# A two-layer recommendation tower on one core: scratch clears between the gathers of the second half, other waits before gathers, W1's gathers moved

## The chip, the core and the metric

The kernel runs on one core of one Trainium2 chip. A core has a matrix engine (TensorE, PE in the profile), a vector engine (DVE), a scalar engine (ACT), GpSimd (POOL) and a queue for plain transfers (SP). Each engine works through its own instructions in order and meets the others through semaphores: an instruction raises one when it is done, and a wait on another engine holds that engine until the count is there. Gathers (indirect DMAs) are issued by POOL and carried out by DMA engines. The metric is the time of one execution in microseconds, as the median of several.

## What is computed

```
e = stack([tbl_f[ids[:, f]] for f in 0..31], axis=1)        # (1024, 32, 64)
xi, xj = e[:, idx_i, :], e[:, idx_j, :]                      # the 496 pairs i < j
left = einsum('bpd,pde->bpe', xi, W)                         # W: (496, 64, 64)
z = sum(left * xj, axis=-1)                                  # (1024, 496)
h = concatenate([z, dense_ctx], axis=1)                      # (1024, 512)
h = maximum(h @ W_top1 + b_top1, 0)                          # 512 -> 512
h = maximum(h @ W_top2 + b_top2, 0)                          # 512 -> 256
y = h @ W_top3                                               # (1024, 1)
```

All values are fp32. Each of the 1024 samples looks up one row of 64 values in each of 32 tables; every pair of fields is combined through its own 64 by 64 matrix; three dense layers follow.

## The kernel before

**Tiling.** The batch is cut into four quarters of 256 samples, two tiles of 128 samples each. The 32 fields are taken as 16 field pairs m = 15 down to 0. A field pair of a quarter needs four gathers (two fields, two tiles; line 625), each of 128 rows of 256 bytes, one row to a partition. So there are 64 gathers to a quarter and 256 in all, counted 0 to 255 here. PE turns the gathered rows over (line 805, four matmuls for a field pair in the profile: every fp32 matmul stands there as two), and ACT copies the result from PSUM to `X` (line 720), two field pairs at a time over most of the program.

**Pieces.** The pair products are made in 248 pieces, 62 to a quarter. A column piece is 8 matmuls of PE at line 840 and one multiply of DVE (line 684 or 680); a row piece is 4 matmuls at line 845 and one multiply at line 692; an "own" piece (2 to a quarter) is 16 matmuls at line 853 and two multiplies at line 672. PE writes a piece to one of three double banks of `left`; DVE reads it, and each multiply raises `multiplied`. PE can be at most three pieces ahead of DVE. Column products are summed by PE (line 866, in turns of eight), row products by ACT (line 737, 16 activations with their reads of the accumulator), by DVE (line 701) or, after the last gather, by POOL (line 642, six steps).

**Dense layers.** Once a quarter's sums are there, its transposes (line 823), four steps of layer 1 (line 884), layer 2 (906) and layer 3 (915) are put in between the pieces of the next quarter; those of the last quarter close the program. Layer 1 needs `W1`, whose rows are also gathered, by four indirect DMAs (line 614) that stand before gather 64.

**What sets the order.** A planner (`Order`) walks through a model of the engines with the constants at the top of the file and writes down one list of steps; every engine issues its part of that list in order. The planner's model of the gathers (`landed`) decides when it takes a field pair.

**What holds the gathers.** Before gather g, POOL waits until `pieces_before(g)` pieces are multiplied: `int((g - 32) * 0.95)` from gather 64 on (in the first quarter also another line, half a piece per gather from gather 16 on, and a limit through the field pairs). So gather 122 waits for 85 pieces, gather 128 for 91, gather 255 for 211. At the start of the third and the fourth quarter POOL also waits for all products two quarters back, since the buffer `rows` holds two quarters.

```
for q in range(QUARTERS):
    if q >= 2:
        pool.wait_ge(multiplied, work_of_quarter[q - 2])
    if q == 1:
        pool.wait_ge(index_loaded, 16)
        for c in range(CHUNKS):
            pool.indirect_dma_start(out=w1_sb[:, c, :], ...)
```

## Time and profile before

| what | value |
|---|---|
| median of 3 runs | 525.97 us (525.26 to 527.53) |
| the profiled execution, its own time | 524.06 us |
| its span (first to last instruction) | 521.9 us |
| PE busy / DVE busy / ACT busy / POOL busy | 423.1 / 336.6 / 337.3 / 279.0 us |
| PE's mean granted clock | 0.935 of full speed |
| gathers | 256, first at 3.4 us, last at 452.1 us |

The profile is one execution. "Busy" is the time in which an engine had an instruction running; for PE the ends are modelled. A wait is put down to the instruction whose semaphore ended it; "issue" stands for a wait that nothing in the profile explains, and "remote" or "another core or an unknown queue" for one whose releaser the profile could not name (there is only one core here). The 2.2 us between span and time lie before the first instruction and after the last.

### The profile page before, as it was taken

The page shows a single profiled execution, that of the slowest core. Times are in us where ns is not written, and L with a number is a line of the kernel's source. Part 1 is how long each engine was busy: PE and PEld are TensorE (multiplying, and loading weights), DVE is VectorE, ACT ScalarE, POOL GpSimd, SP SyncE. Part 2 cuts the span into 40 slices and gives each one's busy share as a digit, 9 for nine tenths or more (in the row PEclk, how much of TensorE's full clock was granted, in tenths as well). Part 3 has the DMA queues.
Part 4 walks back from the last instruction along what each step waited for, and adds up shares of the span by engine and source line. Part 5 has one row for each costly group of instructions (what it writes and reads, how often), then busy time and mean ns, then how long its engine had stood idle before and what let it go on. Part 6 is the DMA issues. An engine that isn't in the chain of part 4 may idle for free.

```text
span 521.9 us, 8845 instructions
## 1 busy us (share of the span) xinstructions
PE 423.1 (81%) x2440; PEld 217.9 (42%) x2440; DVE 336.6 (64%) x293; ACT 337.3 (65%) x2511; POOL 279.0 (53%) x326
## 2 busy tenths in 40 slices
PE   0056697977987879799898897999969788899998
PEld 0033243433534425354444443554424334445546
DVE  0014484666767869376858776787866688698870
ACT  0003584767777867666695786668573897599472
POOL 6747365655646455255455555554455555686510
PEclk9996697979888999799898999999889999999999
DMA  7999900120100010000000000010001000000000
GB/s 136 170 167 166 141 21 20 37 76 22 24 16 21 16 25 15 12 19 23 16 21 20 21 21 22 18 21 21 16 18 23 19 18 18 19 2 1 1 1 1
DMA packets 44680, 18.87 MB, mean 36 GB/s; under 512 B 39764, under 2 KB 40280, under 8 KB 44632
## 3 DMA queue, kind: packets, MB, share of 16 engines
q1 hardware_dynamic: 36120, 8.86, 13.2%
q0 software_dynamic: 8512, 9.45, 8.3%
q8 instruction: 20, 0.33, 0.3%
q14 instruction: 28, 0.23, 0.2%
HBM read 18.29 MB, written 0.00 MB: 35 GB/s over the span
## 4 chain that ended last, share of the span: by engine, by line
PE 50%; ACT 15%; issue 11%; another core or an unknown queue 10%; DVE 9%; POOL 3%; DMA 2%; DVEq 0%; ACTq 0%
PE left L840 15%; PE left L845 15%; ACT row_products L737 14%; PE z_sum L866 9%; PE turned L884 4%; DVE row_products L692 4%; DVE column_products L684 3%; POOL rows L625 3%; PE turned L805 2%; PE turned L906 2%; DVE column_products L672 1%; PE left L884 1%; DMA rows<-in_tbl_dram,ids_sb 1%; ACT X L720 1%
## 5 line engine op out<-in xcount | busy, mean ns | idle before, releaser
L625 POOL DMA_INDIRECT rows<-in_tbl_dram,ids_sb x256 | 242.2, 946 | 204.4 <-issue 64.2
L737 ACT ACTIVATE row_products<-row_products 128x64 f32<-128x64 f32 x1216 | 291.4, 244 | 27.7 <-issue 16.1
L737 ACT ACTIVATION_READ_ACCUMULATOR row_products<-row_products 128x1 f32 x1216 | 231.5, 190 | 20.8 <-issue 19.8
L684 DVE TENSOR_TENSOR column_products<-left,X 128x1024 f32<-128x1024 f32 x104 | 125.1, 1218 | 95.5 <-PE left L840 54.3
L692 DVE TENSOR_TENSOR row_products<-left,rows 128x1024 f32<-128x1024 f32 x120 | 143.1, 1217 | 52.9 <-PE left L845 32.0
L840 PE MATMUL left<-X,w_sb 64*128 64x256 f32 x960 | 138.5, 416 | 26.4 <-DVE row_products L692 8.6
L845 PE MATMUL left<-w_sb,X 64*128 64x512 f32 x480 | 134.9, 658 | 25.1 <-DVE column_products L672 7.9
L840 PEld LDWEIGHTS left<-X,w_sb 64*128 64x128 f32 x960 | 96.3, 201 | 82.9 <-issue 33.3
L866 PE MATMUL z_sum<-column_products,ones_window 128*32 128x512 f32 x512 | 78.7, 661 | 8.3 <-issue 3.9
L845 PEld LDWEIGHTS left<-w_sb,X 64*128 64x128 f32 x480 | 43.3, 197 | 71.7 <-issue 39.4
L720 ACT ACTIVATE X<-turned 128x512 f32<-128x512 f32 (+1 forms) x34 | 19.2, 565 | 77.1 <-issue 27.3
L805 PE MATMUL turned<-ident,rows 128*128 128x128 f32 x128 | 23.4, 307 | 33.9 <-DMA rows<-in_tbl_dram,ids_sb 30.7
L866 PEld LDWEIGHTS z_sum<-column_products,ones_window 128*32 128x32 f32 x512 | 16.5, 118 | 57.6 <-issue 38.0
L701 DVE TENSOR_REDUCE z_nat<-row_products 128x16 f32<-128x1024 f32 x34 | 40.2, 1209 | 0.1
L642 POOL TENSOR_TENSOR row_products<-row_products 128x512 f32<-128x512 f32 (+4 forms) x50 | 30.4, 607 | 12.0 <-DVE row_products L692 8.9
L805 PEld LDWEIGHTS turned<-ident,rows 128*128 128x128 f32 x128 | 14.6, 151 | 52.4 <-issue 49.0
L770 ACT ACTIVATE h<-turned,b_sb 128x256 f32<-128x256 f32 x18 | 7.5, 470 | 30.9 <-PE turned L906 16.0
L672 DVE TENSOR_TENSOR column_products<-left,X 64x1024 f32<-64x1024 f32 x16 | 19.5, 1220 | 12.2 <-remote 9.0
L680 DVE TENSOR_TENSOR column_products<-left,X 128x1024 f32<-128x1024 f32 x16 | 19.5, 1218 | 8.2 <-remote 5.5
L884 PE MATMUL turned<-z,w_sb 128*128 128x256 f32 x96 | 24.0, 393 | 0.0
L884 PEld LDWEIGHTS turned<-z,w_sb 128*128 128x128 f32 x96 | 17.3, 191 | 10.4 <-issue 8.5
L853 PE MATMUL left<-X,w_sb 64*64 64x256 f32 x128 | 17.1, 383 | 1.2 <-issue 1.2
(30 smaller groups left out, 79.5 us busy)
## 6 DMA issues: line engine op xcount, KB each, us to landing
rows<-in_tbl_dram,ids_sb POOLq DMA_INDIRECT x256
w_sb<-in_W_top_dram SPq DMA_DIRECT2D x1, 512.0 KB, 5.6
w_sb<-in_L_rec_W_dram SPq DMA_DIRECT2D x1, 496.0 KB
w_sb<-in_L_rec_W_dram SPq DMA_DIRECT2D x1, 480.0 KB
w_sb<-in_L_rec_W_dram SPq DMA_DIRECT2D x1, 464.0 KB
w_sb<-in_L_rec_W_dram SPq DMA_DIRECT2D x1, 448.0 KB
w_sb<-in_L_rec_W_dram SPq DMA_DIRECT2D x1, 432.0 KB
w_sb<-in_L_rec_W_dram SPq DMA_DIRECT2D x1, 416.0 KB
```

The source lines that it names most:

```text
L625: pool.indirect_dma_start(out=rows[:, q % 2 * QT + t, f * D:(f + 1) * D], out_offset=None, in_=tables[f], in_offset=bass.IndirectOffsetOnA ...
L642: ins = nc.gpsimd.tensor_tensor(to, of[:, :, 0:d], of[:, :, d:2 * d], ALU.add)
L672: ins = nc.vector.tensor_tensor(to[part].rearrange("p o (g b) -> p (o g) b", b=QB), of[part].rearrange("p o (g b) -> p (o g) b", b=QB), X[ ...
L684: nc.vector.tensor_tensor(to, of, X[:, n:n + 2, :].rearrange("p g b -> p (g b)").unsqueeze(1).to_broadcast([P, 2, BANK]), ALU.mult).then_i ...
L692: nc.vector.tensor_tensor(row_products[:, n % ROW_PRODS, :, :], left[:, s, :, :], rows[:, t:t + 1, 2 * D * c:2 * D * (c + 4)].to_broadcast ...
L701: nc.vector.tensor_reduce(z_nat[:, x[2] % (2 * QT), column:column + 16], row_products[:, n % ROW_PRODS, :, :].rearrange("p o (j d) -> p (o ...
L737: ins = nc.scalar.activation(product, product, ACT.Copy, accum_out=z_nat[:, tile, column:column + 1])
L805: ins = nc.tensor.transpose(turned[:, column:column + P], rows[:, q % 2 * QT + t, 2 * D * m:2 * D * (m + 1)], ident[:, :])
L840: ins = nc.tensor.matmul(left[:, s, odd, QB * g:QB * (g + 1)], weights(odd, m, k, 2), X[D * odd:D * odd + D, q % 2 * FP + m, :], start=Tru ...
L845: ins = nc.tensor.matmul(left[:, s, odd, :], X[D * odd:D * odd + D, q % 2 * FP + m, P * t:P * (t + 1)], weights(odd, m, c, 8), start=True, ...
L866: nc.tensor.matmul(z_sum[32 * r:32 * r + 32, :], ones_window[:, 30 - 2 * t:62 - 2 * t], column_products[:, v // 2 % COLUMN_PRODS, v % 2, : ...
L884: ins = nc.tensor.matmul(bank, w1_sb[:, c, n * P:(n + 1) * P], z[:, c, :], start=(begins and c == chunks[0]), stop=(ends and c == chunks[-1]))
```

## The change

**Clears between gathers.** From gather 128 on, POOL clears a scratch tile `pause` of 128 partitions by 320 fp32 columns before every gather, and waits for its own clear to be done (`paused`) before it goes on. The tile is read by nobody. There are 128 such clears.

**Waits before gathers.** `pieces_before` now follows `int((g - 44) * 1.02)`. Gather 64 waits for 20 pieces (30 before), gather 96 for 53 (60), gather 128 for 85 (91), gather 192 for 150 (152), gather 224 for 183 (182), gather 255 for 215 (211).

**W1.** Its four gathers stand one by one before gathers 96, 100, 104 and 108.

**The planner's constants.** A work step costs it 0.83 (0.85), a row sum on DVE 1.3 (1.23) and on ACT 4.0 (3.9), a gather 1.6 from gather 128 on; slack, margin and the spacing of dense layers change. With that the order of the steps on all engines changes; the arithmetic and the number of matmuls and products do not.

```diff
-MLP_APART = 4
-X_WAIT, MLP_WAIT = 10, 16
+MLP_APART = 8
+X_WAIT, MLP_WAIT = 10, 12
-WORK, ... = 0.85, ...
-MULTIPLY, ROWSUM_DVE, ROWSUM_ACT, ... = 1.23, 1.23, 3.9, ...
+WORK, ... = 0.83, ...
+MULTIPLY, ROWSUM_DVE, ROWSUM_ACT, ... = 1.23, 1.3, 4.0, ...
-ACT_SLACK, DVE_SLACK, MARGIN, ... = 0.5, 0.6, 1.0, ...
+ACT_SLACK, DVE_SLACK, MARGIN, ... = 0.5, 1.0, 0.1, ...
-GROUP, AHEAD, APART, LAG = 1, 32, 0.95, 3
+GROUP, AHEAD, APART, LAG = 1, 44, 1.02, 3
+W1_BEFORE = [96, 100, 104, 108]
+PAUSED, PAUSE, PITCH = 128, 320, 1.6
...
-            self.gathered.append(begin + GATHER)
+            self.gathered.append(begin + (GATHER if g < PAUSED else PITCH))
...
-                if q == 1:
-                    pool.wait_ge(index_loaded, 16)
-                    for c in range(CHUNKS):
-                        pool.indirect_dma_start(out=w1_sb[:, c, :], ...).then_inc(w1_loaded, 16)
                 for m in range(FP - 1, -1, -1):
                     for n in range(4):
-                        before = pieces_before(first_gather(q, m) + n)
+                        t, f, g = n // 2, 2 * m + n % 2, first_gather(q, m) + n
+                        if g in W1_BEFORE:
+                            c = W1_BEFORE.index(g)
+                            if c == 0:
+                                pool.wait_ge(index_loaded, 16)
+                            pool.indirect_dma_start(out=w1_sb[:, c, :], ...).then_inc(w1_loaded, 16)
+                        if g >= PAUSED:
+                            nc.gpsimd.memset(pause[:, :], 0.0).then_inc(paused, 1)
+                            pool.wait_ge(paused, g - PAUSED + 1)
+                        before = pieces_before(g)
                         if before:
                             pool.wait_ge(multiplied, before)
```

In the changed file lines 614, 625 and 642 are 627, 638 and 655, and lines 805, 840, 845, 853, 866, 884, 906 and 915 are 818, 853, 858, 866, 879, 897, 919 and 928.

On POOL, from the start of the gathers to the end of the program, this stood before (the last six rows are one row sum, of which there are ten):

```order
L625 DMA rows<-in_tbl_dram,ids_sb 128x64 x64
L614 DMA w_sb<-in_W_top_dram,w_index_sb 128x512 x4
L625 DMA rows<-in_tbl_dram,ids_sb 128x64 x192
L642 TENSOR_TENSOR row_products<-row_products 128x16x32
L642 TENSOR_TENSOR row_products<-row_products 128x16x16
L642 TENSOR_TENSOR row_products<-row_products 128x16x8
L642 TENSOR_TENSOR row_products<-row_products 128x16x4
L642 TENSOR_TENSOR row_products<-row_products 128x16x2
L642 TENSOR_TENSOR z_nat<-row_products 128x16
```

and this stands there now, up to the second gather that has a clear before it:

```order
L638 DMA rows<-in_tbl_dram,ids_sb 128x64 x96
L627 DMA w_sb<-in_W_top_dram,w_index_sb 128x512
L638 DMA rows<-in_tbl_dram,ids_sb 128x64 x4
L627 DMA w_sb<-in_W_top_dram,w_index_sb 128x512
L638 DMA rows<-in_tbl_dram,ids_sb 128x64 x4
L627 DMA w_sb<-in_W_top_dram,w_index_sb 128x512
L638 DMA rows<-in_tbl_dram,ids_sb 128x64 x4
L627 DMA w_sb<-in_W_top_dram,w_index_sb 128x512
L638 DMA rows<-in_tbl_dram,ids_sb 128x64 x20
L632 MEMSET pause 128x320
L638 DMA rows<-in_tbl_dram,ids_sb 128x64
L632 MEMSET pause 128x320
```

The W1 gathers are spread, each gather from 128 on has its clear, and at the end POOL keeps six row sums of ten.

On PE, around the last turning of gathered rows in the program, the order was:

```order
L866 MATMUL z_sum<-column_products,ones_window 32x512 x8
L884 MATMUL turned<-z,w_sb 128x256 x4
L840 MATMUL left<-X,w_sb 128x256 x4
L845 MATMUL left<-w_sb,X 128x512 x4
L805 MATMUL turned<-ident,rows 128x128 x4
L840 MATMUL left<-X,w_sb 128x256 x4
L845 MATMUL left<-w_sb,X 128x512 x6
L805 MATMUL turned<-ident,rows 128x128 x4
L840 MATMUL left<-X,w_sb 128x256 x4
L845 MATMUL left<-w_sb,X 128x512 x4
L866 MATMUL z_sum<-column_products,ones_window 32x512 x8
```

and is now:

```order
L919 MATMUL turned<-h,w_sb 128x256 x4
L858 MATMUL left<-w_sb,X 128x512 x2
L853 MATMUL left<-X,w_sb 128x256 x4
L858 MATMUL left<-w_sb,X 128x512 x2
L818 MATMUL turned<-ident,rows 128x128 x4
L853 MATMUL left<-X,w_sb 128x256 x4
L879 MATMUL z_sum<-column_products,ones_window 32x512 x8
L853 MATMUL left<-X,w_sb 128x256 x4
L858 MATMUL left<-w_sb,X 128x512 x4
L853 MATMUL left<-X,w_sb 128x256 x4
L928 MATMUL turned<-h,w_sb 1x256 x2
```

The last turning, which needs gather 255, stood behind 220 pieces and stands behind 228; the third quarter's layers 1 and 2 (884 and 906, now 897 and 919), of which two steps and all of layer 2 stood behind it, now stand ahead of it.

On ACT, at the end of the program, 16 activations being one row sum, the order was:

```order
L737 ACTIVATE row_products,z_nat<-row_products 128x64 x32
L770 ACTIVATE h<-turned,b_sb 128x256 x2
L737 ACTIVATE row_products,z_nat<-row_products 128x64 x16
L791 ACTIVATE y<-turned 1x256
L737 ACTIVATE row_products,z_nat<-row_products 128x64 x32
L755 ACTIVATE z<-turned 128x512
```

and is now:

```order
L750 ACTIVATE row_products,z_nat<-row_products 128x64 x16
L733 ACTIVATE X<-turned 128x512
L750 ACTIVATE row_products,z_nat<-row_products 128x64 x16
L804 ACTIVATE y<-turned 1x256
L750 ACTIVATE row_products,z_nat<-row_products 128x64 x80
L768 ACTIVATE z<-turned 128x512
```

The last unbroken stretch of row sums on ACT grows from two to five. Over the program ACT has 79 of the 120 row sums (76 before), DVE 35 (34) and POOL 6 (10).

## Rows read from the trace of the kernel before

**Rows 1.** The page: busy times of the engines, and the shares of the chain.

```profile
PE 423.1 (81%) x2440; PEld 217.9 (42%) x2440; DVE 336.6 (64%) x293; ACT 337.3 (65%) x2511; POOL 279.0 (53%) x326
...
PE 50%; ACT 15%; issue 11%; another core or an unknown queue 10%; DVE 9%; POOL 3%; DMA 2%; DVEq 0%; ACTq 0%
```

**Rows 2.** Busy time by stretch; the first line names the columns.

```profile
core 0: us, PE busy (x) PEld busy (x) DVE busy (x) ACT busy (x) POOL busy (x), PEclk, DMA share, GB/s
72.40:117.00 44.60, 36.33 (x176) 16.04 (x172) 27.69 (x25) 29.30 (x216) 27.44 (x29) 0.85 0.16 42
...
210.70:452.10 241.40, 211.34 (x1270) 107.75 (x1272) 171.13 (x149) 171.06 (x1281) 125.77 (x133) 0.96 0.09 19
452.10:506.40 54.30, 53.20 (x324) 28.51 (x322) 49.28 (x43) 42.68 (x330) 33.22 (x61) 1.00 0.01 2
```

**Rows 3.** DVE's waits, 210.7 to 452.1 us: total us, times, longest us.

```profile
DVE column_products L684 <- remote: 10.8, 4, 3.4
DVE column_products L672 <- remote: 9.0, 2, 4.6
DVE row_products L692 <- remote: 8.5, 3, 4.7
```

**Rows 4.** Timeline of POOL from 376 us: start, length, instruction, idle before it.

```profile
376.39 0.95 POOL L625 DMA_INDIRECT rows<-in_tbl_dram,ids_sb  x1 [4.07 <-DVE row_products L692]
...
382.63 0.94 POOL L625 DMA_INDIRECT rows<-in_tbl_dram,ids_sb  x1 [0.30 <-issue]
387.73 0.95 POOL L625 DMA_INDIRECT rows<-in_tbl_dram,ids_sb  x1 [4.15 <-DVE column_products L672]
```

**Rows 5.** Timeline of DVE in the same stretch.

```profile
379.43 1.22 DVE L692 TENSOR_TENSOR row_products<-left,rows 128x1024 f32<-128x1024 f32 x1
385.00 2.46 DVE L672 TENSOR_TENSOR column_products<-left,X 64x1024 f32<-64x1024 f32 x2 [4.36 <-remote]
```

**Rows 6.** Timeline of PE in the same stretch.

```profile
379.00 1.95 PE L853 MATMUL left<-X,w_sb 64*64 64x256 f32 x16
...
387.51 1.71 PE L845 MATMUL left<-w_sb,X 64*128 64x512 f32 x4 [4.05 <-DVE column_products L672]
```

**Rows 7.** Timeline of POOL from 251 us, the first and last of seven gathers.

```profile
251.94 0.94 POOL L625 DMA_INDIRECT rows<-in_tbl_dram,ids_sb  x1 [2.73 <-DVE row_products L692]
...
261.48 0.94 POOL L625 DMA_INDIRECT rows<-in_tbl_dram,ids_sb  x1 [0.30 <-issue]
```

**Rows 8.** Timeline of POOL: gathers 122 and 255, and the first sum.

```profile
210.73 0.95 POOL L625 DMA_INDIRECT rows<-in_tbl_dram,ids_sb  x1 [1.23 <-DVE column_products L684]
...
452.14 0.95 POOL L625 DMA_INDIRECT rows<-in_tbl_dram,ids_sb  x1 [2.82 <-DVE column_products L684]
453.11 3.32 POOL L642 TENSOR_TENSOR row_products<-row_products 128x512 f32<-128x512 f32 x5
```

**Rows 9.** Groups of POOL by shape: count, busy us, mean ns, idle before them.

```profile
L642 POOL TENSOR_TENSOR row_products<-row_products 128x512 f32<-128x512 f32 x10 | 12.7, 1272 | 8.9 <-DVE row_products L692 8.9
...
L604 POOL TENSOR_SCALAR_AFFINE_SELECT ident<-ident 128x128 f32<-128x128 f32 x1 | 0.3, 285 | 0.2 <-POOL ident L602 0.2
L602 POOL MEMSET ident<- 128x128 f32 x1 | 0.2, 205 | 0.3 <-POOLq L947 0.3
```

**Rows 10.** Groups of PE, 210.7 to 452.1 us: count, busy us, mean ns.

```profile
L840 PE MATMUL left<-X,w_sb 64*128 64x256 f32 x512 | 71.0, 401 | 15.9 <-DVE column_products L684 4.7 <-ACT X L720 4.3 <-DVE column_products L680 3.1
L845 PE MATMUL left<-w_sb,X 64*128 64x512 f32 x240 | 66.0, 640 | 11.3 <-DVE column_products L672 4.7 <-ACT X L720 4.5 <-DVE column_products L684 0.8
L866 PE MATMUL z_sum<-column_products,ones_window 128*32 128x512 f32 x286 | 41.9, 652 | 3.8 <-DVE column_products L672 2.4 <-DVE column_products L684 1.5
```

**Rows 11.** The same groups, 452.1 to 506.4 us.

```profile
L845 PE MATMUL left<-w_sb,X 64*128 64x512 f32 x80 | 20.0, 608 | 0.0
L840 PE MATMUL left<-X,w_sb 64*128 64x256 f32 x112 | 15.0, 389 | 0.6 <-DVE column_products L672 0.6
L866 PE MATMUL z_sum<-column_products,ones_window 128*32 128x512 f32 x60 | 7.9, 600 | 1.5 <-DVE column_products L684 1.5
```

## What I expect of the change, before it was run

> **What bounds the kernel now.** I read the page first [rows 1]: PE is busy for 423 of 521.9 us and leads the chain with 50%, but 10% of the chain are waits whose releaser has no name, on a program that has one core. So PE is the bound in part, and something that is not work takes the rest. The table by stretch [rows 2] says where. From gather 122 to gather 255 (210.7 to 452.1 us) PE stands idle for 241.4 - 211.3 = 30.1 us and DVE is busy for 71% of the time. After the last gather (452.1 to 506.4 us), with the same kinds of pieces, PE is idle for 1.1 of 54.3 us and DVE is 91% busy. What differs is that no gathers are issued.
>
> The waits of DVE in the stretch [rows 3] hold 28.3 us in nine waits without a named releaser, of up to 4.7 us. One of them, close up: POOL issues six gathers with only 0.30 us between them, from 376.39 to 382.63 us [rows 4]. PE has finished an own piece at 380.95 us [rows 6], DVE has been free since 380.65, and yet DVE begins that piece at 385.00 [rows 5], 2.4 us after the last gather of the run began. PE, its banks full, starts again at 387.51 and has lost 4 us. PE's signal was there late, not its work. Seven gathers that come as four and three, with a gap between, bring no wait of this kind [rows 7]: they take 9.5 us from first to last start, where seven at the run's pitch of 1.25 us take 7.5. My reading: a long unbroken run of gathers holds back the signals of the other engines until the run has landed, and a gap within it prevents that.
>
> **The clears: what they cost POOL.** The trace has no clear of 320 columns. The one of 128 columns took 0.205 us [rows 9]; if all of that grows with the columns, 320 take 0.51 us, and if most of it is fixed, little over 0.2. A two-input sum of 512 columns took 1.272 us, so at its rate 320 would take 0.80: an upper bound from a dearer kind. I take 0.37. A POOL instruction follows a gather 0.02 us later (452.14 + 0.95 to 453.11) [rows 8]; one that waits for a POOL instruction's signal starts 0.2 us after it [rows 9], and a gather 0.30 us after another [rows 4]: I take 0.28 from a clear to its gather. A gather takes 0.95. The pitch is then 0.95 + 0.02 + 0.37 + 0.28 = 1.62 us, with ends of 1.43 and 2.05. Queued behind each clear is only the next gather, and later POOL's row sums; PE waits for gathers at its turnings. 127 pitches of 1.62 are 206 us, and the stretch now takes 241, so the pace has room.
>
> **What the clears give back.** They turn every run into single gathers with 0.67 us between them. If that ends the held signals, the stretch falls to what PE needs. From above: its busy time as it stands, at the tail's share of 98%, 211.3/0.98 = 215.7 us. From below: the matmuls of the stretch are dearer than those of the tail [rows 10, 11], because PE's issue was slowed and its granted clock was 0.96 rather than 1.00 [rows 2]. At the tail's price lines 840, 845 and 866 would save 71.0 - 512 x 15.0/112 = 2.4, 66.0 - 240 x 20.0/80 = 6.0 and 41.9 - 286 x 7.9/60 = 4.2 us: 198.7/0.98 = 202.8 us. The middle is 209, POOL's own pace is 206, and I add 2 for signals that are still held: 211, a saving of **30.4 us** (25.7 to 38.6). DVE alone, at the 91% of its tail, would need 171.1/0.908 = 188.6; it isn't next. ACT isn't either, with 171.1 busy of 241.4.
>
> **The waits before gathers.** The threshold falls by 6 to 10 pieces between gathers 64 and 128, which no work needs: PE waited for a gather's landing only near the start. In the first half nothing is put between gathers, so earlier release means longer runs. From 72.4 to 117 us POOL has 29 instructions, busy for 27.4 of 44.6 us, and PE is idle for 8.3 us [rows 2]. With the new thresholds POOL finds nearly every wait fulfilled there and about 36 gathers follow on each other. W1's four, a pitch of 1.25 us each, leave this stretch, which gives 5 us of it back; they move to places where POOL waits for pieces anyway, and layer 1 comes 20 pieces after the fourth. Bounds: nothing, or 12 us if PE's idle share there more than doubles. I take **+3 us**. From gather 192 on the thresholds are within four pieces of the old ones. The last gather waits for 215 pieces rather than 211, but the turning that needs it moved from piece 220 to 228, so the lead is 13 pieces, about 19 us, against a landing of 2.4.
>
> **The order.** PE has the same matmuls. Four row sums leave POOL: ACT gets three, of about 3.8 us each, DVE one. Before gather 255 both have time. At the end ACT has five row sums in a row, 19 us, beside 20 pieces at 54.3/37 = 1.47 us, 29 us; that hides, and costs 12 us at most if ACT is late with all. I take **+1 us**, for the last of them before the quarter's transposes. Dense layers in other places cost what they cost before.
>
> **The sum**, against the profiled execution: 521.9 - 30.4 + 3 + 1 = 495.5 us of span; 2.2 us around it make 497.7. The median lies 1.9 us above the profiled execution, so **499.5 us**.
>
> **A rule against this.** DVE's wait of 4.36 us ends with the gathers' landing, not with any work of PE [rows 4 to 6]. The Trainium skill (SBUF — State Buffer, section "SBUF: two separate sides") says that engine ports and DMA ports are disjoint and that a compute operation and a DMA cannot slow each other. By that rule the clears would give nothing and the time would be that of the first rival. The trace disagrees with it at least as far as signals go: 4.36 us without a named releaser in a run of gathers, and none after 452 us. The rival stays for the chance that the common cause is another.
>
> **Rivals.**
> 1. *The number of gathers counts, not the gap.* In a stretch of 241.4 us there are 133 of POOL's gathers, one in 1.8 us; afterwards they come at 1.62 when PE is fast, so the signals would be held as often, only at other places. Against it: the four and three gathers above. Then only the costs stay, 525.97 + 4 = 530 us, or 527 if one or two of the holds go.
> 2. *The clear's own signal is held.* POOL now waits for a signal 128 times. If a hold catches it, the next gather begins only when the last has landed: 2.4 + 0.3 = 2.7 us instead of 1.62. Gathers then bound the end: gather 128 at 210.7 + 3, 127 pitches, 2.4 for landing, 20 pieces of 1.47 with 1 for the turning, 15.5 from the last product to the end: 262 + 127p, and with the 4.1 us above 266.1 + 127p. It decides from p = 1.84 on, and equals the old time at p = 2.05, when 39% of the clears are held. With every second one held, p = 2.16 and the time is 540 us: slower. A clear at the two-input rate (p = 2.05) alone gives the old time. For it: all engines' signals seem to be held, POOL's wait of 4.15 us included [rows 4]. Against: single gathers hold nothing in the trace.
> 3. *The first half's runs cost 12 us, not 3.* 508.5 us, still faster.
> 4. *The clear hides in the gap.* The 0.30 us between gathers may be the sequencer's, beside which a clear costs little; the pitch is then 1.43 and the change does half of what it says: 499.5 + 15 = 514.5 us.
>
> **Chances.** My forecast 0.69, with a range of its own of 488 (38.6 saved, the first half at nothing) to 510 (25.7 saved, ACT's sums at 7); rival 1 0.12; rival 2 0.06; rival 3 0.08; rival 4 0.05. A measurement of this kernel can tell 0.5%, 2.6 us, from no change. Forecast, rivals 3 and 4 and a sliver of rival 1 are faster: 0.83. Rival 1 between 523.3 and 528.6 and a mild rival 2 are the same: 0.07. The rest is slower: 0.10. For 8 in 10 the range has to reach into rival 3 and 4 above, and to a stretch of about 200 us below: 485 to 521.
>
> **What would show it.** Right: starts of gathers from 128 on at 1.55 to 1.75 us; DVE's waits without a releaser in the second half under 8 us instead of 28.3; PE idle under 12 us between the gates at 85 and 211 pieces; the granted clock near 1.00. Wrong: the same holds at the new pitch (rival 1), gaps of over 1.5 us between a clear and its gather without a wait for DVE (rival 2), or PE waiting at its turnings for gathers. If the first half's PE idle time grows by over 8 us, rival 3 was in play.

## The result, and the profile after

| | before | after |
|---|---|---|
| median of 4 runs | 525.86 us (525.26 to 527.53) | 491.04 us (490.39 to 491.57) |
| the profiled execution / its span | 524.06 / 521.9 us | 491.57 / 489.8 us |
| after over before | | 0.9333, 95% interval 0.9307 to 0.9358 |

The changed kernel is faster by 6.7%. The forecast was 499.5 us with a range of 485 to 521; the time lies in the range, 8.5 us below the forecast.

The page of after, first the busy times, the clock by slices, the clears and the last line of the chain (busy us, mean ns, idle before them), against [rows 1]:

```profile
PE 400.6 (82%) x2440; PEld 213.8 (44%) x2440; DVE 336.6 (69%) x294; ACT 344.3 (70%) x2607; POOL 314.8 (64%) x430
...
PEclk9995698677999797999999999999999999999999
...
PE 46%; ACT 5%; issue 2%; DVE 2%; DVEq 0%; ACTq 0%
...
L632 POOL MEMSET pause<- 128x320 f32 x128 | 48.4, 378 | 0.1
```

The 10% of the chain without a named releaser are gone, PE is busy for 22.5 us less with the same 2,440 matmuls, and its clock stays up once the clears have begun. Busy time by stretch, for [rows 2] (us of the stretch, then the engines, granted clock, DMA share, GB/s):

```profile
72.40:117.00 44.60, 22.25 (x124) 11.72 (x122) 19.80 (x17) 21.95 (x160) 26.54 (x29) 0.73 0.11 21
...
225.70:438.00 212.30, 207.31 (x1330) 113.80 (x1328) 188.10 (x165) 184.16 (x1427) 168.69 (x255) 1.00 0.11 21
438.00:474.40 36.40, 34.98 (x240) 18.50 (x240) 33.22 (x29) 32.88 (x264) 20.32 (x37) 1.00 0.01 3
```

Between gather 128 (225.76 us) and gather 255 (437.99) PE now idles for 5.0 us, at clock 1.00. The first half went the other way: from 72.4 to 117 us PE idles for 22.4 us, where it was 8.3. DVE's waits between those two gathers, for [rows 3]:

```profile
DVE row_products L705 <- PE left L858: 12.3, 13, 3.3
DVE column_products L697 <- PE left L853: 5.2, 7, 1.2
DVE row_products L705 <- issue: 4.3, 3, 3.8
```

No "remote" is left among them. POOL's timeline there, for [rows 4] (start, length, idle before):

```profile
376.00 0.95 POOL L638 DMA_INDIRECT rows<-in_tbl_dram,ids_sb  x1 [0.27 <-DVE row_products L705]
376.95 0.38 POOL L632 MEMSET pause<- 128x320 f32 x1
377.60 0.95 POOL L638 DMA_INDIRECT rows<-in_tbl_dram,ids_sb  x1 [0.27 <-POOL pause L632]
378.56 0.38 POOL L632 MEMSET pause<- 128x320 f32 x1
379.45 0.95 POOL L638 DMA_INDIRECT rows<-in_tbl_dram,ids_sb  x1 [0.51 <-DVE column_products L697]
```

Three pitches of 1.60 and one of some 1.88 repeat; the mean is 212.23/127 = 1.671 us. PE's groups from 225.7 to 438 us, for [rows 10, 11]:

```profile
L858 PE MATMUL left<-w_sb,X 64*128 64x512 f32 x270 | 68.6, 609 | 3.2 <-ACT X L733 1.6 <-issue 1.5
L853 PE MATMUL left<-X,w_sb 64*128 64x256 f32 x512 | 67.3, 389 | 0.0
L879 PE MATMUL z_sum<-column_products,ones_window 128*32 128x512 f32 x272 | 32.7, 598 | 0.0
```

The means of 609, 389 and 598 ns are those of the old tail (608, 389, 600), where the old stretch had 640, 401 and 652.

By the pieces at which DVE stands, the 32.1 us of span came from these stretches:

| stretch | before | after | difference | forecast |
|---|---|---|---|---|
| start to piece 85 | 210.5 | 225.0 | +14.5 | +3 |
| piece 85 to piece 211 | 241.4 | 197.5 | -43.9 | -30.4 |
| piece 211 to the end | 70.0 | 67.3 | -2.7 | +1 |

What the first half lost can be seen in one place. The old thresholds no longer break the run, and 14 gathers follow on each other. POOL, then DVE:

```profile
90.36 0.94 POOL L638 DMA_INDIRECT rows<-in_tbl_dram,ids_sb  x1 [3.58 <-DVE column_products L697]
...
106.58 0.94 POOL L638 DMA_INDIRECT rows<-in_tbl_dram,ids_sb  x1 [0.30 <-issue]
```

```profile
94.83 1.21 DVE L714 TENSOR_REDUCE z_nat<-row_products 128x16 f32<-128x1024 f32 x1
110.27 3.49 DVE L705 TENSOR_TENSOR row_products<-left,rows 128x1024 f32<-128x1024 f32 x3 [14.23 <-remote]
```

DVE stands for 14.23 us and goes on 2.7 us after the last of the 14 has left POOL: the wait of [rows 5], three times as long. The size of this loss varies. The same steps up to piece 85 took 219.2, 216.3 and 220.6 us in the traces of a1, m1 and e4 below, on chips 7 and 8.

### The profile page after: what moved, and what is told of

Read it like the earlier page. It is cut to its first block, busy times and chain, and to the rows that moved or that the text cites. A ratio compares the mean times of both kernels' runs of the same rounds, so it can differ in the third digit from the quotient of the medians.

```text
span 489.8 us, 9169 instructions
## 1 busy us (share of the span) xinstructions
PE 400.6 (82%) x2440; PEld 213.8 (44%) x2440; DVE 336.6 (69%) x294; ACT 344.3 (70%) x2607; POOL 314.8 (64%) x430
## 4 chain that ended last, share of the span: by engine, by line
PE 46%; ACT 5%; issue 2%; DVE 2%; DVEq 0%; ACTq 0%
PE left L858 13%; PE left L853 13%; PE z_sum L879 7%; PE turned L897 4%; ACT row_products L750 4%; PE turned L919 2%; PE turned L818 2%; PE left L897 1%; PE left L866 1%; PE turned L928 1%; PE left L919 1%; DVE row_products L705 1%; DVE z_nat L714 0%; DVE column_products L685 0%; ACT X L733 0%
## 5 line engine op out<-in xcount | busy, mean ns | idle before, releaser
L750 ACT ACTIVATE row_products<-row_products 128x64 f32<-128x64 f32 x1264 | 302.5, 244 | 24.3 <-issue 13.6
L750 ACT ACTIVATION_READ_ACCUMULATOR row_products<-row_products 128x1 f32 x1264 | 241.0, 191 | 11.8 <-issue 11.8
L705 DVE TENSOR_TENSOR row_products<-left,rows 128x1024 f32<-128x1024 f32 x120 | 143.3, 1218 | 54.6 <-PE left L858 20.2
L697 DVE TENSOR_TENSOR column_products<-left,X 128x1024 f32<-128x1024 f32 x104 | 125.0, 1218 | 74.1 <-PE left L853 46.4
L853 PE MATMUL left<-X,w_sb 64*128 64x256 f32 x960 | 137.0, 415 | 35.8 <-DVE row_products L705 18.9
L858 PE MATMUL left<-w_sb,X 64*128 64x512 f32 x480 | 128.3, 630 | 15.8 <-DVE column_products L697 12.2
L853 PEld LDWEIGHTS left<-X,w_sb 64*128 64x128 f32 x960 | 94.9, 201 | 92.7 <-issue 32.0
L879 PE MATMUL z_sum<-column_products,ones_window 128*32 128x512 f32 x512 | 64.9, 613 | 1.0 <-DVE column_products L697 1.0
L632 POOL MEMSET pause<- 128x320 f32 x128 | 48.4, 378 | 0.1
L714 DVE TENSOR_REDUCE z_nat<-row_products 128x16 f32<-128x1024 f32 x35 | 41.9, 1209 | 0.0
L879 PEld LDWEIGHTS z_sum<-column_products,ones_window 128*32 128x32 f32 x512 | 13.9, 110 | 36.1 <-issue 29.6
L655 POOL TENSOR_TENSOR row_products<-row_products 128x512 f32<-128x512 f32 (+4 forms) x30 | 18.2, 606 | 8.2 <-DVE row_products L705 6.2
```

What stands on the lines that cost most here:

```text
L632: nc.gpsimd.memset(pause[:, :], 0.0).then_inc(paused, 1)
L697: nc.vector.tensor_tensor(to, of, X[:, n:n + 2, :].rearrange("p g b -> p (g b)").unsqueeze(1).to_broadcast([P, 2, BANK]), ALU.mult).then_i ...
L705: nc.vector.tensor_tensor(row_products[:, n % ROW_PRODS, :, :], left[:, s, :, :], rows[:, t:t + 1, 2 * D * c:2 * D * (c + 4)].to_broadcast ...
L714: nc.vector.tensor_reduce(z_nat[:, x[2] % (2 * QT), column:column + 16], row_products[:, n % ROW_PRODS, :, :].rearrange("p o (j d) -> p (o ...
L750: ins = nc.scalar.activation(product, product, ACT.Copy, accum_out=z_nat[:, tile, column:column + 1])
L853: ins = nc.tensor.matmul(left[:, s, odd, QB * g:QB * (g + 1)], weights(odd, m, k, 2), X[D * odd:D * odd + D, q % 2 * FP + m, :], start=Tru ...
```

## Experiments

A measure that I use below is the **late start**: DVE's start of a piece less the later of PE's last matmul of that piece and DVE's own last end, both from the timeline, summed over all pieces where it is above 0.8 us. Behind gather 128 (so behind 227.3 us) it is 47.7 us before and nothing after; ahead of it, from 30 us on, it is 47.2 us before and 60.1 after. It is more than the waits marked "remote", since many of these waits stand in the views under PE's name: they ended with a signal of PE that had been raised, but came late.

That it is the signal that comes late, and not DVE that fails to take it, the semaphore records of the trace show. The piece of [rows 5] ends on PE at 380.94 us, its signal is recorded at 384.98, and DVE starts at 385.00. In all 39 late starts of before, DVE starts 23 to 25 ns behind the record of a signal of PE. Of the recorded piece signals of PE, 80 of 226 come more than 0.15 us behind PE's last matmul in before, 35 of 205 in after, and none of them behind gather 128. ACT's are late too (18 of 65 row sums in before). DVE's never are, in no trace of the first kind below (251 recorded in before), nor are the signals of the 128 clears in after.

One thing has to be known to read the numbers. **The kernel before took 520 to 526 us in three sets of runs and 426 to 427 us in three others.** The second three were on three chips (1, 13 and 14). Of the first three, two were on chips 7 and 8; the chip of the first comparison is not on record and may be one of them or a third. I call them the first and the second kind. Chips 1, 7, 8, 13 and 14 each stand in one such set only, so the kind may belong to the chip or to its state at that time. Each ratio is to runs of before on the same chip.

**No clears.** The changed kernel's whole plan without the clears, first on two chips of the second kind, then on one of the first.

```
-                        if g >= PAUSED:
-                            nc.gpsimd.memset(pause[:, :], 0.0).then_inc(paused, 1)
-                            pool.wait_ge(paused, g - PAUSED + 1)
```

> The changed kernel with its 128 clears taken out and nothing else: its order of steps, its waits before gathers and the places of W1's gathers stay. My theory (unbroken runs of gathers hold back the engines' signals, and the clears break the runs): the gathers from 128 on come at 1.25 us again in runs, DVE's waits without a named releaser return in the second half (none now, 28 us in the kernel before), and the time goes from 491 to 515-535 us. Rival (the gain came from the new order and the new waits, the clears only keep POOL busy): 488-495 us.

> The changed kernel without its clears again, in the hope of a chip that holds signals (the first such run came to a chip where the kernel before took 427 us and says nothing on holds). If the kernel before takes over 500 us here: by my theory the time is 515-535 us, its own loss in the second half 30 us or more of DVE waits without a releaser; if order and waits made the gain, 485-495 us. If the kernel before takes 427 us: 427 again.

> The changed kernel's plan with all 128 clears left out (the pause tile is never written; the computation is the same). The kernel before takes about 521 to 526 us on one kind of chip and about 427 us on another; both cases are stated. Where before takes over 500 us: theory (the clears end the held signals of the second half, so without them the holds come back from the 128th gather on): 515 to 530 us, with sums of late VectorE starts of some 40 us behind the 128th gather. Rival (the order of the work and the steeper waits did it, not the clears): 485 to 495 us, as the changed kernel. Where before takes about 427 us: 427 within 0.5 per cent by both, as measured already on two such chips.

| run | this | before, same chip | ratio (95%) |
|---|---|---|---|
| e1_no_clears (second kind) | 427.08 | 426.72 | 1.0023 (0.9997 to 1.0048) |
| n1_no_clears (second kind) | 427.26 | 426.37 | 1.0023 (0.9998 to 1.0048) |
| m1_no_clears (first kind) | 512.12 | 520.41 | 0.9828 (0.9765 to 0.9892) |

On the second kind no signal is late (in e1 none of 248 piece signals of PE is recorded more than 0.15 us behind its matmul), and both kernels take the same time. POOL in e1, two rows of a run of 23 gathers at 1.25 us:

```profile
180.10 0.94 POOL L635 DMA_INDIRECT rows<-in_tbl_dram,ids_sb  x1 [0.30 <-DVE column_products L694]
...
207.57 0.94 POOL L635 DMA_INDIRECT rows<-in_tbl_dram,ids_sb  x1 [0.30 <-issue]
```

All of DVE's waits of 1 us and more in sum, of that run's whole span:

```profile
DVE column_products L694 <- PE left L850: 43.0, 17, 31.3
DVE row_products L702 <- PE left L855: 27.1, 27, 5.7
DVE column_products L690 <- PE left L850: 1.6, 2, 1.2
DVE column_products L682 <- PE left L863: 1.0, 2, 0.6
```

There is no "remote" anywhere. On the first kind, m1 has the held signals back behind gather 128. Its waits of DVE there (217.1 to 446.6 us), and one place of POOL and of DVE:

```profile
DVE column_products L694 <- remote: 6.5, 3, 2.9
...
DVE column_products L690 <- remote: 4.7, 2, 3.1
DVE row_products L702 <- remote: 3.0, 1, 3.0
```

```profile
429.81 0.95 POOL L635 DMA_INDIRECT rows<-in_tbl_dram,ids_sb  x1 [0.47 <-issue]
...
433.56 0.95 POOL L635 DMA_INDIRECT rows<-in_tbl_dram,ids_sb  x1 [0.31 <-issue]
```

```profile
430.30 2.35 DVE L694 TENSOR_TENSOR column_products<-left,X 128x1024 f32<-128x1024 f32 x2
435.50 1.23 DVE L694 TENSOR_TENSOR column_products<-left,X 128x1024 f32<-128x1024 f32 x1 [2.85 <-remote]
```

This run is of four gathers only. The kernel before has such places too: after two gathers and a gap of 0.69 us come three, and DVE starts 2.44 us late, POOL and then DVE:

```profile
342.09 0.94 POOL L625 DMA_INDIRECT rows<-in_tbl_dram,ids_sb  x1 [0.69 <-issue]
...
344.58 0.95 POOL L625 DMA_INDIRECT rows<-in_tbl_dram,ids_sb  x1 [0.30 <-issue]
```

```profile
346.52 1.22 DVE L684 TENSOR_TENSOR column_products<-left,X 128x1024 f32<-128x1024 f32 x1 [2.44 <-PE left L840]
```

So a run need not be long to hold a signal, and one gap of 0.69 us between short runs does not always prevent it.

The expectation of m1 had 515 to 530 us by my theory and 485 to 495 by the rival, that order and thresholds did it all. 512.1 is just outside mine, and 17 us from the rival's: 17 late starts between gathers 128 and 255 with 33.4 us in sum (I had said some 40). So on the first kind the order, the thresholds and W1's places bring 1.7% by themselves (interval 1.1 to 2.4%), and the clears, by the difference of the ratios to before (0.9828 - 0.9338, the latter from the next run), 4.9% or 25.5 us; the two ratios come from two chips, each good to 0.7%. The mean pitch of m1's gathers behind gather 128 is (446.56 - 217.08)/127 = 1.807 us; with clears it is 1.671. The gathers come more densely with the clears and hold nothing: the mean rate and the number are excluded as the cause. What stays as the cause is the spacing from one gather to the next. Whether it acts as a gap or as the short pitch within a run (1.25 us against 1.60) the runs do not part, since both changed together.

Three kernels have a trace on each kind, and there the late starts (from 30 us on) can be set beside the difference of the spans: m1 and e1, the same program, 89.9 us of late starts for 81.6 us of span; after and a2, 60.1 for 53.8; m3 and e3 (below), 13.1 for 6.7. The held signals are enough for the whole distance between the kinds.

**The changed kernel again,** on a chip of the first kind and on one of the second.

> The changed kernel itself, run beside the kernel before on the chip of this batch. In the first comparison the kernel before took 526 us and its signals were held in runs of gathers; on the chip of the four runs above it took 427 us and none was held. If this chip is like the first: 491 us against 526. If it is like the second: POOL's pace alone sets the second half. Gather 128 is issued at about 171 us (as in the kernel without clears), 127 pitches of 1.67 us end at 383, and 2.4 + 20 x 1.47 + 16.5 us behind them give a span of 431 us: 431-436 us against 427, a change that is slower by 1-2%. Rival (the clears also free PE there): 425 us or less.

> The changed kernel itself beside the run before it. Where before takes over 500 us: 484 to 492 us again, which makes it the third chip of that kind. Where before takes about 427 us: no hold there to be ended, so only the price of the clears is left: the 128th gather near 172 us, 127 x 1.67 us behind it the last at 384 to 386 us, 436 to 440 us, slower than before by 2 to 3 per cent. The other view (the steeper waits and the order are worth their 8 us there too) has 426 to 431 us.

a1: 486.07 us against 521.28, ratio 0.9338 (0.927 to 0.9406), with the same picture: no late start behind gather 128, 56.0 us ahead of it. a2: 437.89 against 425.94, ratio 1.0284 (1.0262 to 1.0305), as expected (436 to 440). The row of the stretch from gather 128 to 255, of a2 and below it of e1 (no clears):

```profile
171.60:384.00 212.40, 198.43 (x1258) 108.09 (x1256) 177.41 (x155) 174.97 (x1355) 168.84 (x255) 0.98 0.11 21
```

```profile
171.40:364.60 193.20, 189.09 (x1223) 103.69 (x1216) 171.18 (x150) 167.97 (x1303) 119.76 (x128) 1.00 0.12 23
```

Where no signal is held the clears can give nothing; the gathers' pace of 1.67 us takes 212.4 us instead of 193.2, and PE is left with 14 us of idle time instead of 4. This is what the change costs there: 2.8%, against 0.2% without the clears (e1, n1). The expectation of a1 for this kind (431 to 436 us) was too low.

**Smaller clears.** 64 columns instead of 320.

```
-                            nc.gpsimd.memset(pause[:, :], 0.0).then_inc(paused, 1)
+                            nc.gpsimd.memset(pause[:, 0:64], 0.0).then_inc(paused, 1)
```

> The changed kernel with clears of 64 columns instead of 320, at the same 128 places and with the same wait: the pitch of the gathers falls to about 1.45 us. On a chip that holds signals in runs, my theory (a gap is enough, its length matters little) gives 485-493 us, a rival (the mean rate of gathers decides, 1.5 us a gather being what the chip takes) 495-515 us. On a chip that holds none: POOL's pace no longer binds, 426-429 us.

503.87 us against 521.28, ratio 0.9668 (0.9599 to 0.9736), first kind. POOL, and DVE's waits without a releaser behind gather 128 (221.3 to 445.4 us):

```profile
304.69 0.17 POOL L632 MEMSET pause<- 128x64 f32 x1
305.12 0.95 POOL L638 DMA_INDIRECT rows<-in_tbl_dram,ids_sb  x1 [0.27 <-POOL pause L632]
```

```profile
DVE row_products L705 <- remote: 4.9, 3, 2.9
...
DVE column_products L697 <- remote: 2.1, 2, 1.4
...
DVE column_products L693 <- remote: 1.7, 1, 1.7
```

Here some 0.45 us lie between gathers, and 13 late starts of 1 to 3 us come back, 24.4 us in sum. My theory of this run, that any gap is enough (485 to 493 us), is wrong. The time lies in the rival's range (495 to 515), though not for the rival's reason: the mean pitch behind gather 128 is 1.764 us, slower than the 1.671 that holds nothing. The spacing counts by its length: 0.30 us in m1 gives 33.4 us of late starts behind gather 128, 0.45 us gives 24.4, 0.65 us none.

**Clears from gather 32 on,** on a chip of each kind.

```
-                        if g >= PAUSED:
+                        if g >= 32:
...
-                            pool.wait_ge(paused, g - PAUSED + 1)
+                            pool.wait_ge(paused, g - 32 + 1)
```

> The changed kernel with clears from the 32nd gather on instead of the 128th. Where before takes over 500 us: theory (every long run of gathers without clears holds signals, so the first half's holds of some 22 to 34 us go as well): late VectorE starts near zero after the 32nd gather; the gathers' own pace then sets the end, 224 gathers at 1.67 us from about 45 us on end near 420 us, 465 to 476 us in all. Rival (the first half's holds come from something other than the unbroken runs, the preparation's transfers for one): the holds stay, 490 to 500 us. Where before takes about 427 us: 474 us by both, as measured on one such chip.

> The changed kernel with clears from gather 32 on instead of from 128 on, order and waits kept. My theory: the held signals of the first half (DVE waits of 7.3 and 14.2 us between 80 and 111 us, some 35 us after that up to gather 128) go as those of the second half did. POOL's pace then sets the end: 224 gathers at 1.67 us from about 48 us on end at 422 us, and with 2.4 us of landing, 20 pieces of 1.47 us and 16.5 us behind them the span is 470 us: time 468-480 us. Rival (the first half is bound by the weights' arrival and the lower granted clock, not by gathers): 485-492 us.

m3 (first kind): 479.10 us against 520.41, ratio 0.9181 (0.9117 to 0.9245): the fastest kernel of that kind. It has no late start behind 55.4 us. The row of 72.4 to 117 us, where after had 22.25 us of PE, and all of DVE's waits in it:

```profile
72.40:117.00 44.60, 39.41 (x255) 19.75 (x244) 36.59 (x33) 36.11 (x290) 37.13 (x56) 0.96 0.10 22
```

```profile
DVE row_products L705 <- PE left L858: 6.8, 4, 4.4
DVE column_products L697 <- issue: 1.2, 1, 1.2
```

So the first half's holds have the same remedy. What is late next are the gathers. PE's waits over the span of m3, then of e3:

```profile
PE turned L818 <- issue: 41.2, 17, 9.4
PE turned L818 <- DMA rows<-in_tbl_dram,ids_sb: 26.2, 3, 18.6
```

```profile
PE turned L818 <- DMA rows<-in_tbl_dram,ids_sb: 33.2, 4, 18.5
PE turned L818 <- issue: 31.3, 15, 5.4
```

The rows that name the DMA stand in every kernel with about this sum, the start included (29.4 us in e1); what is new are the waits at the turnings under "issue", 3.2 us in e1. From 60 us on, every turning in m3 and e3 that waits over 0.8 us starts 2.4 to 2.6 us after the last gather of its batch was issued: PE turns field pairs that have only just come. e3 (second kind): 473.82 against 426.72, ratio 1.11 (1.107 to 1.1131). The same kernel takes nearly the same time on both kinds (479 and 474 us), though the kernel before differs by 94 us between these two chips: with a gap in front of every gather from 32 on most of what sets the kinds apart is gone. m3 came out 3 us above the upper end of what I expected (476).

**The old kernel with clears.** Order, thresholds and W1 as before, the clears from gather 128 on.

```
+                        g = first_gather(q, m) + n
+                        if g >= PAUSED:
+                            nc.gpsimd.memset(pause[:, :], 0.0).then_inc(paused, 1)
+                            pool.wait_ge(paused, g - PAUSED + 1)
```

> The kernel before with the clears alone: 320 columns and their wait before each gather from 128 on; order, waits before gathers and W1 as before. My theory: the waits without a releaser after gather 128 vanish; POOL's pace of 1.67 us (measured in the changed kernel) puts the last gather at 227.3 + 127 x 1.67 = 439 us at the earliest instead of 452, and the time is 494-506 us. Rival (clears do little without the new order): 518-528 us.

460.39 against 426.72, ratio 1.0769 (1.0729 to 1.0808), second kind, so neither my theory nor the rival was put to the test. Its waits of PE, and one of DVE:

```profile
PE turned L812 <- DMA rows<-in_tbl_dram,ids_sb: 27.2, 2, 18.4
PE turned L812 <- issue: 23.4, 6, 6.0
```

```profile
DVE row_products L699 <- POOL z_nat L649: 12.0, 3, 8.5
```

At the turnings the 23.4 us are new (3.2 in e1), and DVE waits 12.0 us for POOL's ten sums, which begin only after a later last gather; in a2 it waits for none. The clears cost 7.7% with all the rest as it was before and 2.8% with the other edits: the planner's dearer pitch (1.6 us), later turnings, fewer sums for POOL, the new thresholds and W1's places together pay back nearly two thirds of the clears' cost. The runs do not part them. I had missed that this is what they are for.

**Four clears before every fourth gather**: the same mean pace, but runs of four.

```
-                        if g >= PAUSED:
+                        if g >= PAUSED and g % 4 == 0:
+                            for i in range(4):
...
+                                pool.wait_ge(paused, g - PAUSED + i + 1)
```

> The changed kernel with the same 128 clears of 320 columns, but four together before every fourth gather and none before the other three: runs of four gathers at 1.25 us, then a gap of some 2 us, the mean pitch as in the changed kernel (about 1.66 us). It tells the gap from the rate. If the kernel before takes over 500 us here: mean rate decides (1.67 us a gather is enough, 1.45 is not): 484-492 us with no waits of DVE without a releaser after gather 128. The length of unbroken runs decides (four at 1.25 us is short enough, as in the kernel before): the same. Every single gap decides: waits come back and the time is 500 us or more. If the kernel before takes 427 us: as the changed kernel there, 431-436 us.

It was meant to part the gap from the rate, and fell on a chip of the second kind, where nothing is held: 438.70 against 426.37, ratio 1.0289 (1.0255 to 1.0323). I expected 431 to 436 us there, as of a1, and that was too low again. It says only that the price there is the mean pace's (a2 has 1.0284). m1 excludes the mean rate, but what runs of four do on the first kind was not measured as a kernel; the late start behind four gathers in m1, above, speaks against their being free.

**A clear before every second gather from 32 on.** It was to be the version that beats both.

```
-                        if g >= PAUSED:
+                        if g >= 32 and g % 2 == 0:
...
-                            pool.wait_ge(paused, g - PAUSED + 1)
+                            pool.wait_ge(paused, (g - 32) // 2 + 1)
```

> The changed kernel with the clear of 320 columns only before every second gather, from the 32nd on (112 clears). Where before takes over 500 us: with clears before each gather from the 32nd on the gathers themselves set the end (479 us); pairs at about 1.25 and 1.67 us, 1.46 on the mean, end near 48 + 223 x 1.46 = 374 us, off the critical path. Theory (a hold needs a long unbroken run, and two gathers are not one): no late VectorE starts over 0.8 us, 445 to 462 us, the fastest of all kernels here. Rival (each missing clear lets a small hold come, as the 64-column clear let 13 come in the second half): holds of 1 to 3 us by the dozen, 462 to 480 us. Where before takes about 427 us: the theory of the pace alone, 427 to 433 us.

It too fell on the second kind: 441.33 against 425.94, ratio 1.0377 (1.0344 to 1.041), where I expected 427 to 433. The pairs run as computed:

```profile
100.47 0.95 POOL L638 DMA_INDIRECT rows<-in_tbl_dram,ids_sb  x1 [0.27 <-POOL pause L632]
101.73 0.95 POOL L638 DMA_INDIRECT rows<-in_tbl_dram,ids_sb  x1 [0.30 <-issue]
102.67 0.38 POOL L632 MEMSET pause<- 128x320 f32 x1
```

but gather 128 starts at 188.15 us, against 171.6 in a2 and 171.4 in e1. I had compared the gathers' end with the program's end; the first half uses gathers at (171.6 - 48)/96 = 1.29 us each, nearly their bare pitch, and has no room for 1.43. What two gathers in a row do on a chip of the first kind stays open.

**No gathers in the second half.** It leaves out half of the embedding lookups (the third and fourth quarter use the rows of the first and second) and all clears.

```
                 if q >= 2:
-                    pool.wait_ge(multiplied, work_of_quarter[q - 2])
+                    continue
...
-                    pe.wait_ge(rows_gathered[q % 2][m], 16 * 2 * QT * (q // 2 + 1))
+                    pe.wait_ge(rows_gathered[q % 2][m], 16 * 2 * QT)
```

> The changed kernel with no gathers and no clears in the second half: its third and fourth quarter compute with the rows that the first two left, so half of the embedding lookups is left out. It shows what gathers at a pitch of 1.67 us still cost. My theory: nothing but POOL's pace near the end, 484-492 us, first half unchanged. Rival (spaced gathers still hold signals or take from the engines): 480 us or less.

426.91 against 426.72, ratio 0.9994 (0.997 to 1.0017), second kind. Without half the gathers the kernel is no faster there than with them (e1 has 1.0023): on such a chip a gather costs the other engines nothing that can be measured. My expectation was for the first kind, where it was not tried.

## Why the prediction was right, point by point

- **What bounds.** The reading that DVE and PE lose their time to held signals while gathers are issued closely held in every trace of the first kind (m1, a1, e4, m3), and the semaphore records show the signals late. Two details were wrong. The 28.3 us of [rows 3] leave out a tenth wait of 1.7 us, and the late starts there come to 47.7. And a run need not be long: three or four gathers hold a signal for 2 to 3 us. Of the forecast, all marks came out: pitch 1.671 (1.55 to 1.75), no wait without a releaser in the second half (under 8), PE idle for 5.0 us between the gates at 85 and 211 pieces (under 12), clock 1.00.
- **The clear's price.** 1.62 us was forecast and 1.671 measured. The clear took 0.378 us (0.37) and the way to the gather 0.27 (0.28). Without more that is 1.60 us. What was missing is every fourth gather, before which 0.55 us pass: a quarter of 0.28 is 0.07 us, which makes 1.67. Both ends of the bound (1.43, 2.05) were wide.
- **What the clears give back.** The stretch from 85 to 211 pieces was forecast at 211 us and took 197.5. I took the middle of two bounds and added 2 us; the measured time lies 5 us below even the lower bound (202.8, tail prices for every matmul). PE's idle time fell from 30.2 to 5.0 us and its busy time from 211.2 to 192.5, of which some 17 us are dearer matmuls that became cheap (I had 12.6 in three groups, which gave 15), and the rest is other work that lies there now. DVE is busy for 176 of these 197.5 us, 89%, near the 91% of its old tail: little more can come from this stretch.
- **Who earned it.** I gave all of it to the clears. In m1, without them, the same stretch takes 224.9 us: of the 43.9 us, some 16.5 came without the clears and 27.4 with them. A few us of the 16.5 can come from where m1 ran: before took 520.4 us there and not 525.9. So my 30.4 us for the clears was near, and the step that failed is the one that gave order and thresholds nothing but cost there ("+1 us for the order"): over the program m1 gains 1.7% by them, the first half's loss included. e2 against a2 shows that the other edits also keep the clears cheap: 7.7% becomes 2.8%. Why the same work is held less with them (47.7 us of late starts before, 33.4 in m1) stays open.
- **The first half.** +3 us was forecast, +14.5 measured in this trace and +5.8 to +10.1 in those of m1, a1 and e4, set against the one trace of before: rival 3 (12 us, chance 0.08) was in play, by its own mark (PE's idle time between 72.4 and 117 us grew by 14.1 us, over 8). The reason was right, runs without a break, but not the size: I had priced it by nothing and by PE's idle share doubling, and not by the wait's growth with the run's length, 4.36 us for 6 gathers and 14.23 for 14. The kernel before could have suggested it: behind 12 gathers, from 38.7 to 52.5 us, DVE stands for 6.89 us. The run of about 36 gathers did not come; the longest there has 14. How much of the loss is W1's move was not tried by itself.
- **The end.** POOL's sums cost nothing there: 67.3 us for 70.0. ACT's five sums in a row hid.
- **The sum.** Forecast span 495.5, measured 489.8: -13.5 in the second half, +11.5 in the first, -3.7 at the end, so two large errors against each other. That the sum came within 1.7% of the time is luck in part. The remaining 2.8 us of the 8.5 are the time around the span (1.8 for 2.2 us) and the median, which this time lay 0.5 us below the profiled execution and not 1.9 above it.
- **Rival 1** (number, not gap) falls: with the clears the gathers come more densely than in m1 and hold nothing. **Rival 2** (the clear's own signal is held): no gap between a clear and its gather is over 0.56 us, and all 128 signals of the clears are recorded on time. The argument for it misread a row: POOL's wait of 4.15 us in [rows 4] ends with DVE's multiply (387.46 us, recorded at 387.47), so DVE's signal was not held, its work was late. Not all engines' signals are held, but those of PE and ACT. **Rival 4**: the clear does not hide; the pitch goes from 1.25 to 1.60 us, 0.35 us for a clear of 0.378.
- **The rule.** On the second kind nothing was held in runs of gathers at 1.25 us, and e8 priced half the gathers at nothing. The Trainium skill (SBUF — State Buffer, "SBUF: two separate sides") says that neither of a compute operation and a DMA can slow the other; on those chips the traces agree, with ratio 0.9994. On the first kind a gather does delay computing, 14.23 us of wait in a run of 14 gathers, but not by slowing an instruction: DVE's multiply of a column piece takes 1,218 ns in before and in after, and 1,215 in e1. What is late is the signal between engines, of which that section says nothing, so the trace does not contradict what it says of the ports. My prediction took it as speaking against the change, and that was too wide a reading.

What stays open is what differs between the chips, and which part of the path holds the signals. Each execution on record comes with a span and a clock from the profiler, and the traces of the first kind lack part of their semaphore records; whether signals are held in the same way without a profiler no run shows. Not tried on the first kind: clears with the old order, runs of two or of four, the old thresholds in the first half alone.

## What to carry to other kernels

If a wait for an engine ends with the last of a run of transfers rather than with that engine's work, break the run, and size the break by measurement: 0.45 us between gathers took away about a quarter of the late starts here, 0.65 us all of them. Such a break is a toll on the issuing queue: give the scheduler the new pitch, and put it only where the consumer leaves room, or the gathers become the bound (m3, e3). And run before and after on more than one chip before such a change is kept: this one is worth 6.6% on one kind and costs 2.8% on the other.

## What the runs showed that I had not expected

- The same program takes 426 us on three chips and 520 to 526 on at least two others; the difference is held signals alone, as far as the traces show (81.6 us of span and 89.9 us of late starts between e1 and m1). Traces of the gathering kernels on the first kind hold 3,094 to 4,125 records of semaphores, on the second 6,147 to 6,316.
- Where signals are held the matmuls are dearer too, not only later: 640 and 652 ns became 609 and 598 ns. Part of that is the granted clock, 0.96 against 1.00 in these stretches; the traces do not part the two.
- A clear of 64, 128 and 320 columns on POOL takes 0.17, 0.205 and 0.378 us.
